# Routing steps, scatters and the row order of the expert blocks moved in a fused attention and mixture-of-experts kernel

## What is computed

```python
# attention
attn = softmax(clip(q @ k.T * DHEAD ** -0.5, -11, 11)); out = attn @ v
x = x + tanh(g_xattn) * (out @ Wo + bo)      # k with rotary factors cos, sin; inputs layer-normed
# feed-forward, xf = layernorm(x) as rows
scores = sigmoid(xf @ router_w.T); sfc = scores + correction_bias
group_scores = top2(sfc in 8 groups of 8).sum(-1)      # 4 best groups stay
tidx = top8(sfc where its group stays); tw = scores[tidx] / sum * 2.5
routed = sum over experts e of combine[:, e] * (relu2(xf @ up_w[e]) @ down_w[e])
shared = relu2(xf @ shared_up_w) @ shared_down_w
x = x + tanh(g_ffn) * (routed + shared)
```

## Time and profile before

| | us |
|---|---|
| median of 3 runs (from, to) | 2803.03 (2799.3, 2806.53) |
| the profiled execution's own time | 2798.89 |
| its span in the profile | 2796.8 |
| TensorE busy | 2442.9 (87%) |
| VectorE busy | 2122.1 (76%) |
| GpSimd busy | 1953.6 (70%) |
| ScalarE busy | 1166.2 (42%) |
| attention, batches 0, 1, 2 to 7 | 57 to 2110 |
| last routing stage | 2148 to 2339 |
| experts | 2339 to 2797 |

### The profile page before, as it was taken

The page is one execution under the profiler, slowest core; times in us unless marked ns, Lnnn a source line. Parts: engine busy times, 40 slices in busy tenths (PEclk is TensorE's granted clock), DMA queues, the critical chain, the costliest instruction groups (busy, mean ns, idle before and its releaser), DMA issues. The chain is left out here.

```text
span 2796.8 us, 47826 instructions
## 1 busy us (share of the span) xinstructions
PE 2442.9 (87%) x13494; PEld 1474.6 (53%) x13494; DVE 2122.1 (76%) x4773; ACT 1166.2 (42%) x2652; POOL 1953.6 (70%) x2534
## 2 busy tenths in 40 slices
PE   2999999899989988998999899989987885999991
PEld 1555555455545544554555455545543554887781
DVE  4878788777777787778788777777786656688884
ACT  2444444444344434443443444344432322576660
POOL 2877677589768877986798589768876700057776
PEclk9999999899999999999999899999998998999995
DMA  8343343011111111111111111101112405899995
GB/s 306 120 155 108 106 159 106 31 48 61 47 33 64 49 48 45 48 65 45 46 50 48 43 48 59 52 30 65 48 46 95 169 0 189 255 297 324 332 321 151
DMA packets 208567, 301.60 MB, mean 108 GB/s; under 512 B 20066, under 2 KB 177698, under 8 KB 208034
## 3 DMA queue, kind: packets, MB, share of 16 engines
q1 hardware_dynamic: 180194, 230.95, 25.0%
q0 software_dynamic: 24576, 67.14, 7.2%
q10 hardware_dynamic: 3520, 0.27, 0.1%
HBM read 170.37 MB, written 127.93 MB: 107 GB/s over the span
## 5 line engine op out<-in xcount | busy, mean ns | idle before, releaser
L883 ACT ACTIVATE e<-scores 128x1024 f32<-128x1024 f32 x520 | 533.5, 1026 | 949.4 <-PE scores L765 927.5
L975 POOL TENSOR_SCALAR e<-e 128x1024 f32<-128x1024 f32 x520 | 585.0, 1125 | 49.6 <-ACT e L883 6.1
L1118 DVE TENSOR_TENSOR e_sum<-e_sum,e 128x1024 f32<-128x1024 f32 x391 | 586.0, 1499 | 6.7 <-POOL e L975 6.1
L805 PE MATMUL ps_o<-e,v 128*64 128x512 f32 x2088 | 571.7, 626 | 0.4 <-POOL e L975 0.4
L765 PE MATMUL scores<-q_t,k_t 64*128 64x512 f32 x3120 | 515.3, 435 | 31.7 <-ACT affine L862 18.2
L777 PE MATMUL ps_kv<-w,ctx_t 128*128 128x256 f32 x3072 | 513.0, 304 | 25.5 <-DVE rope_s L1101 22.4
L777 PEld LDWEIGHTS ps_kv<-w,ctx_t 128*128 128x128 f32 x3072 | 406.2, 193 | 221.0 <-issue 171.7
L765 PEld LDWEIGHTS scores<-q_t,k_t 64*128 64x128 f32 x3120 | 263.4, 189 | 394.9 <-issue 250.3
L1586 POOL DMA_INDIRECT room<-results_in_blocks,index x256 | 245.3, 958 | 309.6 <-DMA results_in_blocks<-room 229.6
L965 POOL TENSOR_TENSOR k_rot<-rope_c,rope_s 128x64 f32<-128x64 f32 x513 | 355.6, 693 | 55.9 <-DVE rope_s L1101 14.8
L969 POOL TENSOR_TENSOR k_rot<-rope_c,rope_s 128x64 f32<-128x64 f32 x513 | 180.6, 352 | 260.5 <-ACT e L883 260.2
(11 more groups left out here) (269 smaller groups left out, 3477.3 us busy)
## 6 DMA issues: line engine op xcount, KB each, us to landing
w<-w_pairs SPq DMA_DIRECT2D x65, 768.0 KB, 4.6
rows_in_blocks<-room SPq DMA_DIRECT2D x16, 2560.0 KB, 11.3
x_nat<-rows_in_blocks SPq DMA_DIRECT2D x160, 256.0 KB
results_in_blocks<-room SPq DMA_DIRECT2D x80, 512.0 KB
wo<-in_L_xattn_Wo SPq DMA_DIRECT2D x66, 128.0 KB, 4.5
x_nat<-in_ctx SPq DMA_DIRECT2D x64, 128.0 KB, 4.3
down_all<-in_L_ffn_down_w SPq DMA_DIRECT2D x16, 512.0 KB, 7.6
w_pairs<-w_split SPq DMA_DIRECT2D x8, 768.0 KB, 6.9
```

Of the source, the lines that this page charges most:

```text
L805: mm = pe.matmul(ps_o[hh * DH:(hh + 1) * DH, :], v[:, buf, tile, hh * DH:(hh + 1) * DH], e[:, tile % 4, hh * N:(hh + 1) * N], start=(tile ...
L883: act.activation(e[:, c % 4], scores[:, c % 2], ACT.Exp, scale=SCALE).then_inc(s_exp, 1)
L975: pool.tensor_scalar(e[:, c % 4], e[:, c % 4], EXP_HI, EXP_LO, ALU.min, ALU.max).then_inc(s_clip, 1)
L1118: dve.tensor_tensor(total, e[:, 0] if c == 2 else total, e[:, tile % 4], ALU.add).then_inc(s_sum, 1)
```

## The change

1. **Routing on VectorE and TensorE is spread otherwise.** Transposing x is at c = 5 of pairs 2 and 3, logits in pair 4; the bias is added in halves from (1, 6) on; the best groups take pairs 5 and 6 in smaller pieces; the product that makes the gates stands at (6, 6), behind the mask that TensorE's ranking waits for; the slots are finished in pair 0 of the next batch at (0, 1), (0, 4), (0, 5).
2. **Scatters** leave c = 2; places are c = 0, 4, 6, 7 of pairs 1 to 6 and a few others. The rows have a buffer of their own (`rows_now`); ScalarE's `keep_rows` and `keep_all` move to (0, 1) and (1, 1) of the next batch and wait for `sent`, which GpSimd signals at (7, 7) after all 32 scatters have landed.
3. **Last routing stage.** TensorE turns group g + 1 between up and down of group g; three buffers for `x_nat` instead of two; gates are scaled for 28 tiles at once; of 16 of the 32 tiles GpSimd does the product; the experts' first four loads are issued at its end.
4. **Row order in DRAM.** Four neighbouring blocks are interleaved: row = 512 * (block / 4) + 4 * place + block % 4. A load of two blocks then reads 2 KB a partition in one piece, a store of four blocks writes 4 KB. VectorE computes these row numbers with shifts and masks.

```diff
-            places = [(p, c) for p in range(PAIRS) for c in range(0, 8, 2) if (p, c) != (0, 0) and (p, c) < (7, 4)]
-            places += [(7, 3), (7, 4)]
-            places = sorted(places + [(7, 5)])
+            places = [(0, 6), (0, 7)] + [(p, c) for p in range(1, 7) for c in (0, 4, 6, 7)]
+            places += [(3, 5), (7, 0), (7, 2), (7, 4), (7, 5), (7, 6)]
+            places.sort()
...
-                if (p, c) == (2, 7):
+                if (p, c) == (2, 2):
                     router.reciprocals(pool, b - 1)
                 if p is not None and not isinstance(b, int) and (p, c) in places:
                     scatter(b, places.index((p, c)))
+                if (p, c) == (7, 7):
+                    if isinstance(b, int):
+                        pool.wait_ge(cleared, 16 * 2 * PAIRS)
+                    else:
+                        for k in range(GT):
+                            pool.wait_ge(router.scattered[k], (b - 1) * (16 * TOP_K))
+                    pool.sem_inc(router.sent, 1)
...
-                if (p, c) == (6, 4):
-                    router.best_experts(dve)
-                if (p, c) == (6, 7):
-                    router.count_blocks(dve)
                 if (p, c) == (7, 0):
+                    router.overflow(dve)
+                if (p, c) == (7, 1):
+                    router.count_blocks(dve)
                     router.number_blocks(dve, range(0, 3))
-                if (p, c) == (7, 1):
+                if (p, c) == (7, 4):
                     router.number_blocks(dve, range(3, 6))
+                if (p, c) == (7, 5):
                     router.place(dve)
-                    router.slots(dve)
-                if (p, c) == (7, 4):
-                    router.advance(dve)
+                if (p, c) == (7, 6):
+                    router.cross(dve)
...
+                if g + 1 < N_G:
+                    turn(g + 1)
                 pe.wait_ge(s_sq, n + E_S)
...
+            for n, t in enumerate(by_pool):
+                c = pool_cells[:, n % 2]
+                pool.wait_ge(cells_equal, n + 1)
+                pool.tensor_tensor(c, c, router.gate_all[:, t].unsqueeze(1).broadcast_to([P, TOP_K, E_R]), ALU.mult
+                                   ).then_inc(cells_ready, 1)
...
+def four_blocks(dram, i):
+    return dram[i // YC * YC * P:(i // YC + 1) * YC * P, :].rearrange("(p a) n -> p a n", a=YC)
...
-                             xs_dram[i * P:(i + XC) * P, :].rearrange("(a p) n -> p a n", p=P)
+                             four_blocks(xs_dram, i)[:, i % YC:i % YC + XC]
...
-                sp.dma_start(y_dram[i * P:(i + YC) * P, :].rearrange("(a p) n -> p a n", p=P),
+                sp.dma_start(four_blocks(y_dram, i),
                              y[:, i % YR:i % YR + YC]).then_inc(y_stored[i % YR // YC], 16)
```

More of the change, by code:

```diff
@@ L274, in reciprocals, with normalise @@
                            ).then_inc(self.rstd_done, 1)
-    def normalise(self, dve):
+    def normalise(self, dve, half):
         dve.wait_ge(self.rstd_done, self.r + 1)
-        for t in range(GT):
+        if not isinstance(self.r, int) or self.r > 0:
+            dve.wait_ge(self.rows_kept, self.r)
+        for t in range(2 * half, 2 * half + 2):
             st = dve.tensor_scalar(self.x_nat[:, t], self.tile_rows(self.r, t, 1).rearrange("p a n -> p (a n)"),
@@ L455, in slots, with order_slots, rows_of_slots @@
                                            op0=ALU.add, op1=ALU.mult))
-    def advance(self, dve):
+    def order_slots(self, dve):
+        self.ready(dve)
+        dve.memset(self.settle[:], 0.0)
+        for t in range(GT):
+            st = dve.max(self.slot8[:, t], self.slot[:, t])
+        self.mark(st)
+    def advance(self, dve):
+        r = self.r
+        key = self.kept.key[:, r * GT:(r + 1) * GT] if isinstance(r, int) else self.kept.key[:, bass.ds(r * GT, GT)]
+        self.ready(dve)
+        dve.tensor_tensor(self.at, self.at_next[:], self.moved[:], ALU.add)
+        dve.tensor_scalar(self.row[:], self.slot8[:], float(P), -1.0, ALU.mult, ALU.add)
+        self.mark(dve.tensor_tensor(self.moved[:], self.moved[:], new_of(self), ALU.add))
+        self.ready(dve)
+        dve.tensor_copy(key, self.slot8[:])
+        dve.tensor_scalar(self.four[:], self.row[:], 9, 9, ALU.logical_shift_right, ALU.logical_shift_left)
+        dve.tensor_scalar(self.place_in[:], self.row[:], P - 1, 2, ALU.bitwise_and, ALU.logical_shift_left)
+        self.mark(dve.tensor_tensor(self.limit, self.limit, self.moved[:], ALU.add))
+    def rows_of_slots(self, dve):
         r = self.r
@@ L1180, in _ @@
                 sp.wait_ge(router.scattered[k], 16 * TOP_K * N_G)
+            for i in range(0, XR, XC):
+                sp.dma_start(pers.x_nat[:, i:i + XC], four_blocks(xs_dram, i)[:, i % YC:i % YC + XC]).then_inc(kept.x_loaded[i // XC], 16)
             sp.wait_ge(table_in, 16)
@@ L1195, in _ @@
             pool.iota(whole[:], pattern=[[1, E_R]], base=0, channel_multiplier=0).then_inc(made, 1)
+            router.reciprocals(pool, last)
             pool.wait_ge(made, 1)
@@ L1406, in experts @@
         down_loaded = [sem(f"down_loaded_{k}") for k in range(E_R // CHUNK)]
-        x_loaded = [sem(f"xs_loaded_{k}") for k in range(XR // XC)]
+        x_loaded = kept.x_loaded
         y_stored = [sem(f"y_stored_{k}") for k in range(YR // YC)]
```

382 lines of the change are left out of this document (235 added, 147 removed).

## The result

The changed kernel takes 2721.47 us, median of 4 runs (2719.71 to 2726.36), against 2804.24 (2799.3 to 2806.53) for the kernel before: a ratio of 0.971, with a 95% interval of 0.969 to 0.973, so 83 us less. The profiled execution of it took 2726.36, its span is 2724.6, and 72.2 us less than the span before. The two figures differ because the profiled execution of the kernel before was its fastest (2798.89) and that of the changed kernel its slowest.

The account below looks back on a forecast made before the run. The prediction took TensorE to bound the attention, and DMA, then GpSimd's gathers, to pace the experts. Attention -86, last routing stage -21 and experts -6 gave -113: 2686 profiled, 2690 on the median's basis, 8-in-10 range 2652 to 2742.

Parts of the forecast that it names:

- R1: Rival, chance 0.25: half the gain; GpSimd's backlog at pair ends moves the wait to k_rot, ranking still costs the clock; 2742 or 2720.
- the scatters' wait goes when they leave step 2: Attention: without the scatter in step 2, o_n starts about 1.1 us earlier and TensorE's wait of 0.93 a pair goes.
- the 8 of the routing: Attention: batch 1, with routing but no scatters, gains 8 us from the shorter ranking wait and the rope_s wait in pair 7.
- a sign of being wrong: Attention: TensorE waits at L795 for k_rot, listed among what would show the forecast wrong; no size given.
- the early half of the spread routing: Attention, pairs 2 and 4: half a turning of x, and the logits (some 2 us), offset by savings; net 0 in each.
- ranking and clock: Attention, pair 6: the ranking's wait falls from 3.3 to about 1.5 and the clock is kept, -5.5; without the clock -2.
- the last routing stage: After the attention: TensorE's turn fills the wait for the squares, 15.4 a group against 20.3; -21 us, GpSimd's help bringing almost nothing.
- Pair 7: Attention: slots move to the next batch, the rope_s wait of 2.3 and 0.9 to 1.7 of the slow stretch go; -3.2.
- handover and preloading: Start of the experts: issuing the first four loads earlier saves 2.5 at the handover and 2.8 in the first DMA-bound stretch.
- the larger pieces: Expert stage, first 32 blocks: pieces above 1 KB are at most 11% cheaper for DMA; -1 us, ends 0 and -2.
- R3: Rival, chance 0.03: longer store pieces slow the experts' gathers to 2.0 us each, deciding from 1.71; 2790 to 2870.
- R4: Rival, chance 0.03; the text given does not say what it claims.

Follow-up runs that it names:

- no_c0_even: Changed kernel with the scatters of step 0 of pairs 2, 4 and 6 moved to step 1 of pairs 1, 3 and 5: a batch 252.6 us against 255.5.
- places_alone: Kernel before with only the scatter of step 2 moved to step 7 in pairs 1 to 6: 2825.01 us against 2803.85, a single run each.
- places_c2: Changed kernel with the scatters of step 7 (pairs 1 to 6) back at step 2: batches 2 to 7 take 1527.8 us against 1523.4.
- masks_alone: Kernel before with only the best eight moved to step 1 of pair 6 and the gates' product to step 6: batches 2 to 7 1546.2 us against 1564.5.
- no_help: Changed kernel with VectorE alone ordering all 32 tiles, without GpSimd's product: 2863.52 us against 2859.95 measured together.
- plain_rows: Changed kernel with DRAM rows in plain order, so 1 KB pieces again: 2862.26 us against 2859.95 measured together.
- no_preload: Changed kernel with the first four loads issued by the expert stage again: 2863.55 us against 2859.95 measured together.

## Why the forecast came out as it did

The forecast was 2690, the range 2652 to 2742, the result 2721.5. The direction and the range held, but the gain was 83 where 113 was forecast, and the result lies in the bracket of rival R1 (2712 to 2750, held at 0.25). By the two profiled executions 72 came of 113, and the shortfall has one main place, the scatters in batches 2 to 7.

*Wrong: that the scatters' wait goes when they leave step 2.* The prediction let 0.93 us go in every pair, about 5 a batch beside the 8 of the routing, and said of the new steps that "what covers it is that TensorE needs k_rot only a step later", with 0 to 0.5 a pair near pair ends. Set against batch 1 of the same kernel, batches 2 to 6 took 9.8 more before and 11.8 more after: the scatters' cost rose by 2 instead of falling by 5. This is an estimate, and good to some 2 us, since batch 1 takes 243.7 to 245.6 in the six profiles with this attention; pairs 1 to 6 agree to 0.1 in it. So the rise is uncertain, but that the 5 did not come is not. Together with the routing's 9.0 (forecast 8) that makes the 7.0 a batch instead of 13.0. The step later does cover in pairs 1, 3 and 5, where that cost fell from about 3 to 1.2 in all; in pairs 2, 4 and 6 it rose from 3.3 to 5.7. The prediction had looked at single scatters (1.06) and not at what else stands on GpSimd in the same steps of even pairs, seven power operations of 3.6 us. It had also put the wait for o_n down to the scatter in every pair, though pair 2 of batch 1 waited 0.8 without one. That the scatters near these operations are what costs is shown by no_c0_even (the even pairs' cost from 5.7 to 1.7, that of pairs 1, 3 and 5 from 1.2 to about 3); that the power operations are what makes even pairs different is read from the timeline, and no run moved them. places_alone shows the size without the rest: moving the scatters that way costs 21 us by itself. Beside the change's own routing it gains some 4 (places_c2).

R1 named this backlog and the place of the new wait (k_rot), which the prediction had also listed as a sign of being wrong, but saw it at the end of all pairs. R1 gave 2720 to 2742, and its lower end is what came, in part by luck: of its terms the clock behind the ranking (lost) and the last stage (14) did not come, and its 36 for the loop was 41.

*Wrong in size: the early half of the spread routing.* In batch 1, without scatters, pair 2 rose from 29.1 to 30.8 and pair 4 from 28.7 to 30.1, pair 5 fell from 30.1 to 28.2 and pair 3 stayed. The prediction priced the turning in pair 2 and the logits in pair 4 at about the 0.9 of wait that each pair was to save; they cost 1.7 and 1.4. In pair 2 TensorE then waits for VectorE as well (window 352.7:383.5 of the changed kernel):

```profile
PE ps_kv L819 <- DVE rope_s L1183: 0.7, 1, 0.7
PE ps_y L293 <- DVE x L1175: 0.5, 1, 0.5
```

Pairs 6 and 7 made up for it in batch 1, with -6.4 and -3.7.

*Right: ranking and clock.* Pair 6's wait was to fall from 3.3 to about 1.5 and the clock to be kept. masks_alone measured 1.48 and a clock of 1.00; in the full change 0.3 is left. The prediction's doubt came from a misreading: it had waits of 1.35 in the last routing stage followed sometimes by the low clock, but behind all eight of them the clock is 1.00, and the low one (0.80 in the product up) stands behind four of the five waits of 2.13 and more. Pair 7: -3.1 measured, -3.2 forecast, and by the way forecast. The wait of 2.3 went, and with it the low clock behind it, some 3 us of which half came back; the products of the pair end 28.0 us after its start instead of 31.5. Batch 1: -9.0, forecast -8.

*Right: the last routing stage.* -20.8 against -21, with TensorE's groups at 15.4 and the tile at 1.89 instead of 1.97. Two errors of 3 cancel in it: TensorE ended 180.4 us after the last batch (forecast 177.5, the first product up took 9.07), and VectorE's tail behind it was 27.1 (forecast 29 to 30). The Trainium skill, "SBUF — State Buffer", section "Who interferes with whom", says that a VectorE instruction with two SBUF inputs contends with a GpSimd one that reads SBUF, and that on this chip tensor_reduce does not. The trace agrees: the comparison takes 1.26 beside GpSimd's product and 0.69 alone, the reduction 0.67 and 0.69. The help gives 0.28 a tile, 3 us behind the last product (no_help).

*Wrong: handover and preloading were counted twice.* The 2.5 for the first wait and the 2.8 for 1 MB less were two terms, though both are the same transfer time of a stretch that DMA binds from its first load. Measured: from the first load's issue to block 32 46.9 us before (windows of 2339.35 to 2386.2), 42.9 after, 4.0 less, of which plain_rows puts 1.0 on the larger pieces (forecast 1) and no_preload about 3 on preloading. A further 0.8 came between block 32 and the first gather, and the gathers' stretch was 2.6 longer, so that 2.2 is left of 6.

*Not seen: R3 and R4.* The gathers did not go beyond 1.28 us each in the first profile, far below 1.71, and packets are larger: the pieces merged and did not push the gathers aside. On chips 0 and 15 the gathers took 1.6, in the kernel with plain rows as well, so that is not R3 either.
